# Two-layer attention and expert kernel: the routing of the next sequence moved into the second experts

## The reference, cut to what matters

```python
def layer0(xn):                       # xn = layernorm(x), x: 8 x 1024 x 128
    c_q, c_kv = xn @ W_DQ + b_DQ, xn @ W_DKV + b_DKV
    attn = softmax(q k^T / sqrt(160))       # 8 heads
    ...
    logits = xn @ router_w.T                # top 2 of 8 experts
    out += dense_w[:, e] * ((silu(x @ w_gate[e].T) * (x @ w_up[e].T)) @ w_down[e].T)
x = x + attention0(xn) + experts0(xn)
xn = layernorm(x)
x = x + flow_attention(xn) + experts1(xn)   # linear attention; top 4 of 8, clipped SwiGLU
```

## Time and profile before

| | |
|---|---|
| median of 3 runs | 2558.47 us (2558.06 to 2561.96) |
| the profiled execution | 2557.68 us, its span 2555.9 us |
| PE busy | 2315.6 us, 91% |
| DVE busy | 1982.7 us, 78% |
| ACT busy | 1660.5 us, 65% |
| POOL busy | 737.2 us, 29% |
| mean granted TensorE clock | 0.962 of full speed |

### The profile page before, as it was taken

The page is one execution under the profiler, slowest core; times in us unless marked ns, Lnnn a source line. Parts: engine busy times, 40 slices in busy tenths (PEclk is TensorE's granted clock), DMA queues, the critical chain, the costliest instruction groups (busy, mean ns, idle before and its releaser), DMA issues.

```text
span 2555.9 us, 64898 instructions
## 1 busy us (share of the span) xinstructions
PE 2315.6 (91%) x25503; PEld 1656.1 (65%) x25503; DVE 1982.7 (78%) x3435; ACT 1660.5 (65%) x3050; POOL 737.2 (29%) x621
## 2 busy tenths in 40 slices
PE   6989989899898998989989899898998989988998
PEld 3667566665666666766667666676666766666665
DVE  6778877788778887787876878868778687786986
ACT  4866558665686656775567755767457684585845
POOL 2220432205322052221522215212253023530234
PEclk8999999999999999999989999999999999999999
DMA  7110211103111121111211112111121112211022
GB/s 250 51 42 2 106 54 43 42 19 104 39 45 39 43 84 35 47 38 43 88 32 49 34 47 88 33 48 30 63 76 34 44 30 76 68 35 49 19 78 63
DMA packets 99124, 141.35 MB, mean 55 GB/s; under 512 B 11523, under 2 KB 60620, under 8 KB 98316
## 3 DMA queue, kind: packets, MB, share of 16 engines
q1 hardware_dynamic: 90636, 120.41, 14.9%
q0 software_dynamic: 8192, 16.79, 2.3%
HBM read 101.84 MB, written 31.13 MB: 52 GB/s over the span
## 4 chain that ended last, share of the span: by engine, by line
PE 60%; DVE 20%; issue 10%; ACT 8%; POOL 1%; SPq 0%; DVEq 0%; DMA 0%; ACTq 0%; POOLq 0%
PE ps L1552 11%; PE ps L1723 7%; DVE neg_max L1209 7%; PE ps L1745 6%; PE ps L1760 6%; PE ps L1559 6%; PE ps L1634 5%; ACT probs L821 4%; PE ps L1656 3%; PE ps L1509 2%; DVE ffn L1352 2%; PE ps L1573 2%; DVE probsT L1219 2%; DVE key_low L977 2%; PE ps L1645 1%
## 5 line engine op out<-in xcount | busy, mean ns | idle before, releaser
L1209 DVE TENSOR_REDUCE neg_max<-ps 128x1 f32<-128x1024 f32 x512 | 622.2, 1216 | 85.9 <-PE ps L1723 79.3
L821 ACT ACTIVATE probs<-ps,neg_max 128x1024 f32<-128x1024 f32 x512 | 577.0, 1127 | 76.1 <-DVE neg_max L1209 72.8
L1552 PE MATMUL ps<-shared,w_split 128*128 128x512 f32 x1536 | 471.1, 443 | 18.2 <-ACT ffn L872 11.6
L1745 PEld LDWEIGHTS ps<-ident,probs 64*128 64x128 f32 x8192 | 338.4, 145 | 172.3 <-issue 134.7
L706 POOL TENSOR_TENSOR probs<-ffn,shared 128x512 f32<-128x512 f32 x208 | 287.7, 1383 | 410.6 <-DVE ffn L1352 183.4
L1745 PE MATMUL ps<-ident,probs 64*128 64x64 f32 x8192 | 364.7, 231 | 41.4 <-issue 28.5
L1552 PEld LDWEIGHTS ps<-shared,w_split 128*128 128x128 f32 x1536 | 288.9, 193 | 165.0 <-issue 62.9
L872 ACT ACTIVATE ffn<-ps,room_of_gate 128x512 f32<-128x512 f32 x256 | 175.0, 683 | 270.5 <-PE ps L1552 270.5
L1723 PE MATMUL ps<-shared,query_a 64*128 64x512 f32 x1024 | 268.6, 521 | 84.5 <-ACT probs L821 62.2
L1760 PE MATMUL ps<-probsT,latent 128*32 128x128 f32 x8192 | 327.0, 279 | 12.9 <-DVE o_latent L1202 12.7
L805 ACT COPY probsT<-ps 128x512 f32<-128x512 f32 x512 | 303.2, 592 | 25.8 <-PE ps L1745 24.3
(11 more groups left out here) (231 smaller groups left out, 3501.7 us busy)
## 6 DMA issues: line engine op xcount, KB each, us to landing
w_split<-w_parts SPq DMA_DIRECT2D x132, 256.0 KB, 2.6
shared<-gate_rows SPq DMA_DIRECT2D x64, 512.0 KB, 4.4
y_rows<-probs SPq DMA_DIRECT2D x40, 256.0 KB, 2.2
x_in<-in_x SPq DMA_DIRECT2D x9, 512.0 KB, 4.1
out<-x_mid SPq DMA_DIRECT2D x8, 512.0 KB, 3.2
ffn<-in_gate_up SPq DMA_DIRECT2D x1, 2048.0 KB, 8.7
probsT<-in_gate_up SPq DMA_DIRECT2D x1, 2048.0 KB, 13.4
w_down<-in_down SPq DMA_DIRECT2D x2, 1024.0 KB
```

The lines of the kernel that those rows point to most:

```text
L821: nc.scalar.activation(probs[:, t % 3, :], banks(2 * (t % 2)), ACT.Exp, bias=neg_max[:, t % 4:t % 4 + 1], accum_out=row_sum[:, g % 2, t % ...
L1209: nc.vector.tensor_reduce(neg_max[:, t % 4:t % 4 + 1], banks(2 * (t % 2)), X, ALU.max, negate=True).then_inc(max_ready.sem, 1)
L1552: mm = nc.tensor.matmul(ps[:, bank, :], w_split[:, f % CHUNK_SLOTS, h, k * P:(k + 1) * P], tokens[:, half], start=(part == 0), stop=(part ...
L1745: mm = nc.tensor.transpose(ps[:, turn_bank(t, c), k * HQ:(k + 1) * HQ], probs[rows, t % 3, k * P:(k + 1) * P], ident[rows, rows])
```

## The change

The routing of sequence n+1 is done in the second experts of sequence n. DVE does `route_two` at units 10, 17, 18, 20 and 22 (2, 2, 3, 2 and 2 steps), with room for the pairs in `probs`; PE does the prefix counts at unit 20; DVE does `places` at units 20 and 23 to 27. The four pair operations are all on DVE. Sequence 0 has its routing in its first run as before. The 16 scatters stand first in POOL's list of a first run, ahead of the input's add; SP loads the sorted tokens ahead of the next input. The first four blocks of tokens are turned in step `TOKENS_STEP` = 33 into bank 1, before the last tile. In the first run `high` copies are on DVE for 28 of 32 tiles, as in the second run. The gathered rows are multiplied and added by POOL in four operations on 128x1024 right after the gathers, in place of DVE's 16 steps. The semaphores of DVE's chained steps now count without a restart per sequence. The core of the diff:

```diff
-COMBINE_STEP = PERIOD + 16
+TOKENS_STEP = QUAD_STEPS + T_LAG - 2
+
+
+NEXT_ROUTE = {10: 2, 17: 2, 18: 3, 20: 2, 22: 2}
+NEXT_PREFIX = 20
+NEXT_PLACES = {20: 1, 23: 4, 24: 3, 25: 3, 27: 4}
...
+def token_bank(q):
+
+    return 1 if q == 0 else 2
...
-    run, i = divmod(t, NT * QUAD)
-    return i % 2 == 0 if run == 0 else i % 8 == 3
+    return t % 8 == 3
...
+        next_pairs = [probs[:, 1, i * BANK:(i + 1) * BANK].rearrange("p (n e j) -> p n e j", n=NT, e=E) for i in range(2)]
+        next_room = probs[:, 1, 0:BLOCKS * E].rearrange("p (j e) -> p j e", e=E)
...
+                sp.wait_ge(scattered.sem, scattered.at(b, 16 * 2 * NT))
+                sp.sem_inc(rows_complete.sem, 1)
+                if index > 0:
+                    sp.wait_ge(down_done.sem, down_done.at(b, 0))
+                sp.dma_start(xs, x_rows[:, :].rearrange("(j p) d -> p j d", p=P)).then_inc(xs_loaded.sem, 16)
                 sp.wait_ge(norm_ready.sem, norm_ready.at(b, 0))
                 sp.wait_ge(x_taken.sem, x_taken.at(b, 1))
                 sp.dma_start(x_in[:, :, :], ins["x"][bass.ds((index + 1) % BATCH, 1), :, :].rearrange("a (n p) d -> p (a n) d", p=P)
                              ).then_inc(x_loaded.sem, 16)
-                sp.wait_ge(scattered.sem, scattered.at(b, 16 * 2 * NT))
-                sp.sem_inc(rows_complete.sem, 1)
-                sp.dma_start(xs, x_rows[:, :].rearrange("(j p) d -> p j d", p=P)).then_inc(xs_loaded.sem, 16)
...
-                pool.wait_ge(pairs_made.sem, pairs_made.at(b, 1))
-                nc.gpsimd.tensor_tensor(pair_b, pair_b, earlier[:, :, :].unsqueeze(1).to_broadcast([P, NT, E, E]),
-                                        ALU.mult).then_inc(pairs_step.sem, 1)
-                pool.wait_ge(pairs_step.sem, pairs_step.at(b, 1))
-                nc.gpsimd.tensor_tensor(pair_a, pair_a, pair_b, ALU.add).then_inc(pairs_ready.sem, 1)
...
-                pool.wait_ge(pos_ready.sem, pos_ready.at(b, 1))
+                pool.wait_ge(pos_ready.sem, pos_ready.at(b, 0))
...
+                pool.wait_ge(shares_ready.sem, shares_ready.at(b, 1))
+                for part in gathered:
+                    pool.wait_ge(part.sem, part.at(b, 16 * 2 * NT // GATHERS))
+                for k, share in enumerate((r_s1, r_s2)):
+                    nc.gpsimd.tensor_tensor(y_pair[:, k, :, :], y_pair[:, k, :, :],
+                                            share[:, :].unsqueeze(2).to_broadcast([P, NT, D]), ALU.mult
+                                            ).then_inc(combined.sem, 1)
...
+                pool.wait_ge(x_taken.sem, x_taken.at(b, 1))
+                for k in range(2):
+                    pool.wait_ge(combined.sem, combined.at(b, 2 + k))
+                    nc.gpsimd.tensor_tensor(x_mid[:, :, :], x_mid[:, :, :], y_pair[:, k, :, :], ALU.add
+                                            ).then_inc(combined.sem, 1)
                 inverse_deviation(b, 2, slice(0, NT - 1))
...
+                    if w == TOKENS_STEP:
+                        tokens_high(0)
...
+                    yield from ranks(logits_first, pairs)
...
-                    if 0 < w < PLACES_STEP - 1 or PLACES_STEP + PLACES_STEPS <= w < QUAD_STEPS + 1:
+                    if index == 0 and 0 < w < PLACES_STEP - 1:
...
-                    if COMBINE_STEP <= w < COMBINE_STEP + 2 * NT:
-
-                        n, choice = divmod(w - COMBINE_STEP, 2)
-                        if choice == 0:
-                            dve.wait_ge(x_taken.sem, x_taken.at(b, 1))
-                            dve.wait_ge(gathered[n * GATHERS // NT].sem,
-                                        gathered[n * GATHERS // NT].at(b, 16 * 2 * NT // GATHERS))
-                        else:
-                            dve.wait_ge(combined.sem, combined.at(b, 2 * n + 1))
-                        nc.vector.scalar_tensor_tensor(x_mid[:, n, :], y_pair[:, choice, n, :],
-                                                       (r_s1, r_s2)[choice][:, n:n + 1], x_mid[:, n, :],
-                                                       ALU.mult, ALU.add).then_inc(combined.sem, 1)
...
+                    if index + 1 < BATCH:
+                        if u == min(NEXT_ROUTE):
+                            dve.wait_ge(down_done.sem, down_done.at(b, 1))
+                            dve.wait_ge(rows_stored.sem, rows_stored.at(b, 16))
+                        for _ in range(NEXT_ROUTE.get(u, 0)):
+                            next(next_route, None)
+                        for _ in range(NEXT_PLACES.get(u, 0)):
+                            next(next_place, None)
...
+            def prefixes(made):
+
+                pe.wait_ge(chosen_ready.sem, chosen_ready.at(made, 1))
+                counts = 2 * P + (NT + 1) * E
+                nc.tensor.matmul(ps[:, 7, 2 * P:counts], before[:, :],
+                                 chosen[:, :, :].rearrange("p n e -> p (n e)"), start=True, stop=False)
+                for m in range(NT):
+                    mm = nc.tensor.matmul(ps[:, 7, 2 * P + (m + 1) * E:counts], ones,
+                                          chosen[:, m, :].unsqueeze(1).to_broadcast([P, NT - m, E]),
+                                          start=False, stop=(m == NT - 1))
+                mm.then_inc(prefix_mm.sem, 1)
...
-                pe.wait_ge(low_copied.sem, low_copied.at(b, NT * QUAD))
-                pe.wait_ge(high_copied.sem, high_copied.at(b, on_dve(NT * QUAD)))
-                pe.wait_ge(blocks_ready.sem, blocks_ready.at(b, 1))
+                pe.wait_ge(blocks_ready.sem, blocks_ready.at(b, 0))
                 first = {}
-                tokens(0)
...
+                    if j == TRANSPOSE_LAG:
+
+                        pe.wait_ge(low_copied.sem, low_copied.at(b, NT * QUAD))
+                        pe.wait_ge(high_copied.sem, high_copied.at(b, on_dve(NT * QUAD)))
...
+                    if index == 0 and g == 0 and i == NT // 2 - 1:
+                        prefixes(None)
...
+                    if u == NEXT_PREFIX and index + 1 < BATCH:
+                        prefixes(b)
...
```

More of the change, by code:

```diff
@@ L418, in two_layer_kernel @@
         rows_zeroed = signal("rows_zeroed")
[L419 to L426, removed]
+        chosen_ready = signal("chosen_ready", 1, start=1)
+        prefix_mm = signal("prefix_mm", 1, start=1)
+        prefix_taken = signal("prefix_taken", 1, start=1)
+        pos_ready = signal("pos_ready", 1, start=1)
+        blocks_ready = signal("blocks_ready", 1, start=1)
         scattered = signal("scattered", 16 * 2 * NT)
@@ L836, in tokens_high @@
                     act.wait_ge(xsT_mm.sem, xsT_mm.at(b, q + 1))
-                    nc.scalar.copy(xs_parts[0][:, q % 2 * BANK:q % 2 * BANK + n], ps[:, 2, 0:n]).then_inc(xs_high_ready.sem, 1)
-                tokens_high(0)
+                    nc.scalar.copy(xs_parts[0][:, q % 2 * BANK:q % 2 * BANK + n], ps[:, token_bank(q), 0:n]
+                                   ).then_inc(xs_high_ready.sem, 1)
+                for w in range(QUAD_STEPS + T_LAG):
+                    attention_step(w)
+                    if w == TOKENS_STEP:
+                        tokens_high(0)
                 for j in range(BLOCKS + BLOCK_DOWN_LAG):
@@ L1184, in experts_add @@
                             ps[:, 6 + c, :].rearrange("p (n d) -> p n d", d=D), ALU.add).then_inc(y_added.sem, 1)
-                route, place, weights = route_two(), places(), route_weights()
+                route, place = route_two(None, (pair_a, pair_b)), places(None, 7, cmp_room)
+                next_route, next_place = route_two(b, next_pairs), places(b, 7, next_room)
+                weights = route_weights()
                 def split_low():
@@ L1279, in tokens_low @@
                     at = slice(q % 2 * BANK, q % 2 * BANK + n)
-                    nc.vector.tensor_tensor(xs_parts[1][:, at], ps[:, 2, 0:n], xs_parts[0][:, at].bitcast(F32), ALU.subtract
-                                            ).then_inc(xs_low_ready.sem, 1)
+                    nc.vector.tensor_tensor(xs_parts[1][:, at], ps[:, token_bank(q), 0:n], xs_parts[0][:, at].bitcast(F32),
+                                            ALU.subtract).then_inc(xs_low_ready.sem, 1)
+                for w in range(QUAD_STEPS + T_LAG):
+                    attention_step(w)
+                    if w == TOKENS_STEP:
+                        tokens_low(0)
                 def outputs(q):
@@ L1288, in outputs @@
                                           ps[:, 5 + q % 2, 0:len(part) * D]).then_inc(ys_ready.sem, 1)
-                assert next(route, "end") == "end" and next(place, "end") == "end"
+                assert index > 0 or next(route, "end") == "end" and next(place, "end") == "end"
                 for j in range(BLOCKS + BLOCK_DOWN_LAG + 1):
@@ L1459, in _ @@
                         queries_rest(u - NEXT_KEYS)
+                    if index + 1 < BATCH:
[6 more added lines that the diff above has]
+                            next(next_place, None)
```

(15 more changed lines are left out.)

105 lines of the change are left out of this document (47 added, 58 removed).

## The result

The changed kernel takes 2564.99 us (median of 20 runs, 2557.61 to 2573.26), the kernel before 2559.88 (20 runs beside it, 2554.54 to 2564.1): a ratio of 1.002, interval 1.0011 to 1.003. It is slower by 5 us. Forecast were 2545 and a gain of 0.5%. The profiled execution took 2566.54 us with a span of 2564.8.

A forecast was written before the change was run, and what follows sets the result against it. PE was taken to bound the second experts' second half, three engines the attention loop. Gains of 73 us less costs of 60 gave -13 on the profiled 2557.7, so 2545; range 2518 to 2576.

The forecast's parts named there:

- signs that I had named as refuting: PE's idle before the prefix counts missing or far longer than 2.6 to 5.2 us, or first-run beat staying near 1.95.
- (g): Second experts: granted clock falls after PE's idle at unit 20, costing 2.3 us a sequence, bounds 0 and 5.4.
- (f): Second experts of sequences 0 to 6: prefix counts 1.73 us plus PE idle 4.0 us, 1.4 of it from POOL's holding.
- (a): First runs of sequences 1 to 7: without routing and with the second run's copy split, 39 us gained.
- (b): Second runs: 16 combining steps leave DVE for POOL, 2.9 us gained per sequence, 23 in all.
- (d): First-run start: POOL's scatters and the later input add and load are covered, cost 0; uncovered, 20 us.
- (h): Second experts, units 23 to 27: twelve small place operations fit DVE's free time, cost 0, bound 0.5 a sequence.
- (c): After the second run's tile 31: sorted tokens turned earlier, first block starts sooner, 1.4 us a sequence, 11 in all.
- (e): Sequence 0's first run: routing kept, with more pair operations and copies on DVE, costs 4 us once, bounds 0 and 8.
- Rival 1: PE's wait for `chosen`: idle 5.2, clock 5.4, giving 2575; decides from 9.9 us a sequence; chance 0.22.

The follow-up runs named there:

- e5: Changed kernel with 6 products that nobody reads ahead of PE's wait for `chosen`: 2540.32 us, 0.992 to the kernel before.
- e6: Changed kernel with ranking spread over units 19 to 24, prefix counts at unit 25, places at 25 to 28: 2516.85 us, 0.9838 to the kernel before.
- e9: e6 with the routing's row maximum and subtraction at unit 18 instead of unit 10: 2530.21 us, 0.988 to the kernel before.
- e10: e6 once more, unchanged, as partner of e9 on the same chip: 2515.37 us, 0.9836 to the kernel before.
- e1: Changed kernel with PE's prefix counts at unit 23 instead of 20: 2536.67 us, 0.9892 to the kernel before.
- e8: Changed kernel with the first run's high copies split half and half between ACT and DVE again: 2597.86 us, 1.0152 to the kernel before.

## Why the prediction was wrong

The sign hung on seven sequences' clock. With 5.2 in place of 2.3 the forecast's own sum is -13 + 7 x 2.9 = +7, against 8.9 between the spans. With the 4.6 that stand at the counts alone it is -13 + 7 x 2.3 = +3. None of the signs that I had named as refuting came: the idle was there, the beat was 1.85. The fall to 0.5 was named, its length was not.

- **(g), the step that failed.** The step is the size of the clock term, 2.3 us a sequence. The mechanism was named: an idle of 4 us in one piece is followed by a granted clock of 0.5, where PE is the bound. The size was taken from the starts of second runs, as a mean of 2.3. There the clock is low for 3.4 or 6.8 us within the windows; at the counts it is low for 6.8 us in two sequences and 10.2 in five. The bound 5.4, from the start of a first run, was almost the truth. e5 puts what hangs on this wait at 4.2; the remaining 1.0 a sequence is lost in e5 too. Why the clock stays low longer here isn't shown.
- **(f) held.** Idle 3.65 to 3.92 for 4.0. One pair operation was held by POOL, 1.1 us where 1.4 was taken: the second took 1.77 us beside POOL's product (1.67), the others 0.68, 0.69 and 0.67. The fourth ran inside the record of a product of POOL (949.43) that took 2.24 us instead of some 1.27. The sum, a reduction, took 0.69 beside the same product. By the Trainium skill (SBUF — State Buffer, "Who interferes with whom") two-SBUF-input operations and GpSimd's reads exclude one another, and a reduction is not held; these times agree.
- **An edit left out of (f).** I started the count at unit 17 and costed the two steps of unit 10 at nothing without saying so. The subtraction is of 128x64, but it too has two SBUF inputs and took 1.26 us beside POOL; 0.79 us of it reached PE at unit 16, 5.5 us in seven sequences. Other waits shrank by nearly as much, so that the idle came out right in sum, by luck.
- **(a), (b), (d), (h) held**, (c) was 1.2 for 1.4 a sequence. (d): the 16 scatters run on POOL from 993.27 to 1013.3, and none of them is in the chain of work that ended last. **(e)** was +2.6 for +4.
- **Rival 1**, slower at 2575 by 5.2 us idle and 5.4 clock, is what happened with the lesser idle: 11.2 a sequence, past its point of decision of 9.9. I had written against it that both ends would have to meet. One and a bit was enough.
- **The last stage of sequence 7** has no routing and is 2.4 us longer in after: its clock lost 7.1 us and not 3.4, its idle is the same (11.9 and 12.1). In e6, e9 and e10 it is 0.4 to 0.5 us shorter. So the clock's falls also differ by some us between kernels that do the same work in this stage; what moves them isn't shown.

## What to carry to other kernels

Where one engine has no gaps, a step that is moved under its cover must be ready before the engine arrives. Cost the wait at its length plus the work at half clock behind it: here another 4 to 5 us for one wait of 4. If the wait can't be moved, try filling it: six products that nobody reads made this kernel 25 us faster. And choose the place by the engine that feeds the bound one, here DVE, rather than by TensorE alone: e6, laid out by that, is 1.6% faster than the kernel before. e6 moved the steps and the counts together, so how much each gave isn't known.

## What the hardware showed that I had not expected

- One idle of 3.65 to 3.92 us was met by a granted clock of 0.5 in all seven sequences of after, for 6.8 us in two and 10.2 us in five, nearly all of it with PE busy; e5, where products fill the wait, has none there. In e1, 3.4 us of idle in pieces of about 1.1 left the clock at 1.00 around the counts.
- Length alone doesn't decide. The wait at unit 16 is 2.24 us in seven sequences each of after, e10 and e1 to e8, and the clock fell at 27 of these 70 (one of after's seven, sequence 2: 0.61 in 939 to 943; three of e5's). Where the same wait is 1.45 us, in before, in e9 and in every sequence 7, it fell at none of 26. But e9's 1.56 to 1.58 us ahead of the counts were followed by a fall in six sequences of seven.
- DVE's 128x64 subtraction of two SBUF operands took 1.26 us in unit 10, where it started 0.08 us after a product of POOL (920.17, 1.27 us) and ended within 0.1 us of it, and 0.21 in all eight first runs of before. How small an operation is doesn't protect it.
- 128x384 products in full precision are two instructions each in the record and took 0.65 us.
